# Block-sparse attention on one core: a block's row maxima from two products of 256 keys in place of one product with two runs of 192

## What is computed

```
inner = einsum('bhlqd,bhlkd->bhlqk', mq, exp_k) * scale      # 3 blocks: own and neighbours
first_band = einsum('bhlqd,bhkd->bhlqk', mq, kb[:, :, 0]) * scale
last_band = einsum('bhlqd,bhkd->bhlqk', mq, kb[:, :, -1]) * scale
aw = softmax(concatenate([first_band, inner, last_band], axis=-1), axis=-1)
```

## Time and profile before

| what | value |
|---|---|
| median of 3 runs | 1995.65 us |
| the profiled execution, its own time | 1994.81 us |
| its span, first to last instruction | 1993.0 us |
| mean granted TensorE clock | 0.901 of full speed |
| TensorE products busy (PE) | 1702.8 us, 85% |
| TensorE weight loads busy (PEld) | 1374.2 us, 69% |
| VectorE (DVE) | 1202.6 us, 60% |
| ScalarE (ACT) | 879.8 us, 44% |
| GpSimd (POOL) | 631.8 us, 32% |

### The profile page before, as it was taken

The page is one execution under the profiler, slowest core; times in us unless marked ns, Lnnn a source line. Parts: engine busy times, 40 slices in busy tenths (PEclk is TensorE's granted clock), DMA queues, the critical chain, the costliest instruction groups (busy, mean ns, idle before and its releaser), DMA issues. The chain is left out here.

```text
span 1993.0 us, 34683 instructions
## 1 busy us (share of the span) xinstructions
PE 1702.8 (85%) x12738; PEld 1374.2 (69%) x12738; DVE 1202.6 (60%) x2634; ACT 879.8 (44%) x1734; POOL 631.8 (32%) x636
## 2 busy tenths in 40 slices
PE   5749999999999359789999949959996399999991
PEld 4624766666666238767888825549995399999991
DVE  4657677767771466746555548756674655556543
ACT  3300566667668035344333336644442044444433
POOL 1340022201112336547777613223330113323111
PEclk9965799999999559999999979989998599999996
DMA  5795133333310573013444331010114213433214
GB/s 188 259 168 70 33 73 76 87 80 70 78 40 14 175 273 129 26 57 65 72 72 72 55 130 64 1 45 22 43 43 153 58 20 95 130 95 93 78 14 170
DMA packets 141796, 173.77 MB, mean 87 GB/s; under 512 B 72298, under 2 KB 108608, under 8 KB 141632
## 3 DMA queue, kind: packets, MB, share of 16 engines
q1 hardware_dynamic: 102400, 116.06, 19.3%
q0 software_dynamic: 32128, 51.82, 12.4%
q10 hardware_dynamic: 7104, 3.67, 1.2%
HBM read 109.20 MB, written 65.54 MB: 88 GB/s over the span
## 5 line engine op out<-in xcount | busy, mean ns | idle before, releaser
L583 DVE TENSOR_REDUCE att_neg_max<-att_m_ps 128x1 f32<-128x320 f32 x496 | 234.6, 486 | 131.0 <-PE att_m_ps L410 123.2
L410 PE MATMUL att_m_ps<-att_k,att_q 96*128 96x384 f32 x496 | 229.9, 475 | 28.2 <-DMA att_k<-qk 21.0
L1754 PE MATMUL silu_h_ps<-silu_xT,silu_w_part 128*128 128x320 f32 x1536 | 237.2, 313 | 1.2 <-DVE silu_xT L1850 0.9
L1754 PEld LDWEIGHTS silu_h_ps<-silu_xT,silu_w_part 128*128 128x128 f32 x1536 | 227.5, 189 | 2.4 <-DVE silu_xT L1850 1.3
L410 PEld LDWEIGHTS att_m_ps<-att_k,att_q 96*128 96x128 f32 x496 | 103.9, 209 | 137.1 <-DVE att_neg_max L583 87.2
L1719 POOL DMA_INDIRECT summed<-silu_y,all_table x40 | 63.8, 1594 | 256.6 <-DVE silu_y L1890 149.9
L548 ACT ACTIVATE att_prob_f<-att_b_ps 128x1024 f32<-128x1024 f32 x64 | 65.5, 1023 | 172.3 <-PE att_b_ps L434 172.3
L1480 POOL DMA_INDIRECT part<-gelu_y,all_table x72 | 118.6, 1648 | 60.1 <-DVE gelu_y L1601 48.9
L1766 PE MATMUL silu_y_ps<-silu_w_part,silu_h_part 128*128 128x256 f32 x960 | 116.5, 283 | 2.2 <-DVE silu_w_part L1866 2.2
L1766 PEld LDWEIGHTS silu_y_ps<-silu_w_part,silu_h_part 128*128 128x128 f32 x960 | 115.9, 192 | 2.5 <-DVE silu_w_part L1866 2.5
L1509 PE MATMUL gelu_h_ps<-gelu_wu_part,gelu_xT 128*128 x402 | 110.1, 409 | 2.7 <-DVE gelu_wu_part L1608 2.5
(11 more groups left out here) (315 smaller groups left out, 3961.0 us busy)
## 6 DMA issues: line engine op xcount, KB each, us to landing
experts_w<-in_dram SPq DMA_DIRECT2D x24, 1024.0 KB
qk<-qkv_part POOLq DMA_DIRECT2D x32, 512.0 KB, 3.4
att_k<-qk SPq DMA_DIRECT2D x192, 64.0 KB, 2.3
att_q<-qk SPq DMA_DIRECT2D x168, 64.0 KB, 3.1
v<-qkv_v POOLq DMA_DIRECT2D x8, 544.0 KB, 4.9
att_v<-v SPq DMA_DIRECT2D x8, 544.0 KB, 4.3
qkv_x<-in_dram SPq DMA_DIRECT2D x8, 512.0 KB, 5.9
merge_c<-context SPq DMA_DIRECT2D x8, 512.0 KB, 5.2
```

The source lines that it names most:

```text
L410: nc.tensor.matmul(bank[:, 0:2 * LOCAL].rearrange("p (a n) -> p a n", a=2), q[b][0:MROW, x, :], local_and_global(b, x), start=True, stop=T ...
L583: ins = nc.vector.tensor_reduce(neg_max[p % 2][:, x:x + 1], m_ps[u % 2][:, 0:LOCAL + 2 * BLK], AX.X, ALU.max, negate=True)
L1754: mm = nc.tensor.matmul(h_ps[u % 2][a][:, :], w12_part[f % RING][wp][:, a, k, :], xT[s][xp][:, k, rows], start=(i == 0), stop=(i == 3 * KD ...
```

## The change

The one product of a "b" unit becomes two, with the same weights. The first reads 256 keys in a row, from one block further left (from key 0 for block 1), into columns 0 to 255 of the bank. The second reads the 256 columns from 4096 on (first block, last block, 128 zeros) and writes them directly behind the three blocks that count: at column 256, or at 192 for block 1, where it overwrites a block that isn't wanted. Only the second raises `m_done`. VectorE reduces 320 columns as before, now starting at column 64 (0 for block 1). The key buffer grows by 64 columns, and GpSimd clears 128 columns instead of 64.

```
-    LOCAL = 3 * BLK
+    LOCAL, WIDE = 3 * BLK, 4 * BLK
...
-        k = [m.sb(f"k{i}", [P, T + LOCAL], F32R) for i in range(2)]
+        k = [m.sb(f"k{i}", [P, T + WIDE], F32R) for i in range(2)]
...
-        def local_and_global(b, l):
-
-            own = k[b][0:MROW, (l - 1) * BLK:(l - 1) * BLK + LOCAL]
-            rows, cols = own.ap
-            return bass.AP(own.tensor, own.offset, [list(rows), [T - (l - 1) * BLK, 2], list(cols)])
+        def first_key(l):
+
+
+            return max(l - 2, 0) * BLK
+
+        def first_maximum(l):
+            return (l - 1) * BLK - first_key(l)
...
-                    nc.tensor.matmul(bank[:, 0:2 * LOCAL].rearrange("p (a n) -> p a n", a=2), q[b][0:MROW, x, :],
-                                     local_and_global(b, x), start=True, stop=True).then_inc(m_done, 1)
+                    at = first_key(x)
+                    nc.tensor.matmul(bank[:, 0:WIDE], q[b][0:MROW, x, :], k[b][0:MROW, at:at + WIDE], start=True, stop=True)
+                    at = first_maximum(x) + LOCAL
+                    nc.tensor.matmul(bank[:, at:at + WIDE], q[b][0:MROW, x, :], k[b][0:MROW, T:T + WIDE],
+                                     start=True, stop=True).then_inc(m_done, 1)
...
-                    ins = nc.vector.tensor_reduce(neg_max[p % 2][:, x:x + 1], m_ps[u % 2][:, 0:LOCAL + 2 * BLK], AX.X,
+                    at = first_maximum(x)
+                    ins = nc.vector.tensor_reduce(neg_max[p % 2][:, x:x + 1], m_ps[u % 2][:, at:at + LOCAL + 2 * BLK], AX.X,
                                                   ALU.max, negate=True)
...
-                nc.gpsimd.memset(k[b][0:MROW, T + 2 * BLK:T + LOCAL].bitcast(F32), 0.0).then_inc(padded, 1)
+                nc.gpsimd.memset(k[b][0:MROW, T + 2 * BLK:T + WIDE].bitcast(F32), 0.0).then_inc(padded, 1)
```

## The result

The changed kernel takes 2014.42 us (median of 5, 2009.57 to 2021.21) against 1996.01 us before, a ratio of 1.0086 with a 95% interval of 1.0070 to 1.0102: 18 us slower. Run again later beside 23 executions of the kernel before it took 2015.28 (ratio 1.0087, 1.0071 to 1.0104). The forecast was 2020 within 2007 to 2026. The profiled execution took 2014.42, its span is 2012.6 and its mean granted clock 0.904, a little above the 0.901 of before.

What follows compares the result with a forecast made beforehand. The prediction took TensorE, without a gap in attention's woven steps, as the bound. It added 17.6 us at the high clock, 4.0 in round 1 and 3.9 in pair 0, 25.5 in all, to 1994.81: 2020, range 2007 to 2026.

Steps and rivals of the forecast that it cites:

- The price of a unit: On TensorE, two products of 256 columns instead of one of 384 cost 0.06 us more at high clock, 0.11 at low.
- columns with a hidden load: On TensorE, 128 more columns set a unit's price; the second weight load runs during the product before it.
- What lies on the path: In woven steps at high clock, two units count in each band or full step: 0.12 us a step.
- Pair 0: Maxima before the woven steps, low clock: two loops side by side, 70 units, 70 / 2 x 0.11 = 3.9 us.
- the prediction's sum: Time added in attention: 17.6 us at high clock, 4.0 in round 1 at low clock, 3.9 in pair 0's maxima; 25.5.
- the 17.6: High-clock woven steps: of 390 units 96 are hidden and 294 count, 294 x 0.06 = 17.6 us.
- No penalty for two runs: The old product's two key runs cost nothing that joining could return: next start 0.28 us later either way.
- The clock in round 1: Round 1 at the low clock: all 36 units count, 36 x 0.11 = 4.0 us, with the rise in the band steps.
- some 7 us later, in the same band steps: Sign of being right: the granted clock rises in round 1's band steps, some 7 us later than before.
- before the band steps: Sign of being wrong: the clock rises in round 1 ahead of its band steps.
- The rival of 13%: Clock rises at the start of round 1, saving 10.2 us there: 12.5 us slower in all, 2007.3; chance 13%.

Runs made afterwards that it cites:

- the one product of 512: Changed kernel with its two products of 256 columns replaced by one product reading two runs of 256: 2014.80 us, ratio 1.0103.
- the repetition: The changed kernel run again without any edit, beside later executions of the kernel before: 2015.28 us, ratio 1.0087.
- The two changed kernels with fillers: Changed kernel with 36 products ahead of pair 0's maxima: 2016.76 us; with these and 90 more before round 1: 2016.63 us.
- the 384 run: Kernel before, its product reading one run of 384 keys instead of two runs of 192: 1996.49 us, ratio 1.0006.
- the two fillers in the kernel before: Kernel before with 36 products ahead of pair 0's maxima: 1996.90 us; with these and 90 more before round 1: 1997.14 us.
- the burst: 16 products of 512 columns into a free bank just ahead of round 1: 1991.74 us in the kernel before, 2013.78 in the changed one.
- The kernel with 64 columns fewer a unit: Kernel before with two products, of 192 and 128 columns, in place of one of 384: 2007.46 us, ratio 1.0066.

## Why the prediction was right, and where it was not

**The price of a unit** (0.06 at the high clock, 0.11 at the low) held: 0.34 for 0.28, 1.38 for 1.27. Its reason, columns with a hidden load, held for 256 columns and is shown by the one product of 512.

**What lies on the path** held: the first and third unit of a band step, the first and fourth of a full step. 0.12 each makes 2.76 for 23 steps; the rounds grew by 2.8. Round 7 grew by 2.2 (19 steps, 2.3). Pair 0 grew by 3.6 and 3.4, with 3.9 said. In the prediction's sum 1.6 us of the 17.6 fall into the end of round 1 (26 units at 0.06), so everything outside round 1 was to cost 25.5 - 4.0 - 1.6 = 19.9 us. It measured 19.9 in the first trace and 19.7 in the repetition.

**No penalty for two runs** held. The rule of the Trainium skill (PSUM — Partial Sum Buffer, Specifications), that any non-contiguous access pattern slows matmuls significantly, stands there in the row on PSUM's cachelines and doesn't say which operand it means. It didn't show for this read of two long runs, while the write to PSUM is one run in both kernels: 337, 444 and 691 ns contiguous against 337, 443 and 690. The Trainium skill's line that a load overlaps only products in other row groups (TensorE: Matmul & The Clock Gate, The mechanism) doesn't hold here: the second load starts at 305.52, 0.12 before its own product, while the first one on the same rows streams. The same section also names a load into a background weight buffer as one that is pulled ahead, and with that the trace agrees; the prediction quoted only the first half.

**The clock in round 1 is the step that failed.** The prediction put 4.0 us on the low clock there and the rise "some 7 us later, in the same band steps"; with the 1.6 above, round 1 was to grow by 5.6 us. It shrank by 5.0 in the first trace and grew by 0.7 in the repetition. The clock rose in the full steps, the third and the seventh, at 206.3 and 220.1 us where the kernel before has 226.2. A clock that rises "before the band steps" is one of the prediction's own signs of being wrong. The two changed kernels with fillers had the rise in the fifth and the seventh step, the one of 512 columns in the seventh. The kernel before, the 384 run and the two fillers in the kernel before all had it in the tenth. The rival of 13%, a rise at the start of round 1, took off the whole 10.2 us of the ten steps; the executions took part of it, each another part. The price of a unit at the low clock (0.11) was right, only fewer units paid it.

So the mechanism of the price was right, and the number is in the range, at the lower edge of the 2014 to 2026 that the prediction gave to its sum. The sum missed 6 to 7 of its 25.5 us, and that it missed no more is in part luck. In the first trace round 1 came out 10.6 us under what was forecast for it, and 4.7 of them were lost outside what the sum covers: 0.9 ahead of pair 0 and 3.8 outside attention. Nor is the rise all that differs between executions. With the rise held in the burst, the changed kernel still spread over 8.6 us (2010.17 to 2018.77), against 11.6 and 8.8 without it, and what follows attention took between 1334.4 and 1342.2 us in the 14 traces.

Open is why the clock rises where it does: why pair 0's maxima don't get it back once it has fallen although TensorE's records are dense, and what in the kernels with 512 columns a unit brings the rise forward. The kernel with the two products in round 1's full steps alone had it at 32.9 us in its trace, so it isn't those products by themselves. No run told these apart.

## What to carry to other kernels

Price a product by the distance of starts, by its columns, but never below what its weight load takes (here 0.11 us at the high clock, about what 256 columns take). In this kernel, products of that size added only their extra columns, and products below it lost even with fewer columns. When a stretch at the low clock lies next to the edit, ask whether the edit moves the rise, in both directions, and give that its own term. A short burst of products whose results nobody uses, ahead of a dense stretch, can be worth more than it costs: 6.8 us for 10.8 here.

## What the runs showed of the hardware that I had not expected

The same program had its clock rise at 9.7 and at 25.5 us after the first score product in two executions, and round 1 was 5.6 us longer in the second; every kernel that has single 384-column products outside round 1's full steps had it at 32 to 35. The kernel with 64 columns fewer a unit kept the clock low more than twice as long as before (79.4 us against 33.7) in its profiled execution, with TensorE's records touching for all of the 79.4. Sixteen products of 512 columns brought the clock up within 6.5 us, and 36 products of identity with identity within 4.3.
